# Six local attention layers: lower bound of the norms on ACT, rotation products stored head by head, and mix, output projection and MLP one unit later

## What is computed

```python
q, k, v = split(x_shifted @ Wqkv)
q = l2norm(q) * qs;  k = l2norm(k) * ks          # l2norm: t / max(|t|, 1e-12)
q = q * cos * scale + rotate_half(q) * sin * scale   # k with 1 / scale
p = softmax(8 * q @ k_near.T + mask)             # own window and the one before
x = x + (p @ v_near) @ Wo
xn = layernorm(x_shifted) * g + b
a, gate = split(xn @ W1 + b1)                    # 2 x 341
x = x + (a * gelu(gate)) @ W2 + b2
```

## Time and profile before

| | us |
|---|---|
| median of 3 runs | 3254.74 |
| lowest and highest | 3243.23, 3268.76 |
| profiled execution, its own time | 3245.79 |
| its span, first to last instruction | 3244.0 |
| PE busy in the span | 3124.8 (96%) |
| DVE busy | 3011.8 (93%) |
| POOL busy | 2636.1 (81%) |
| ACT busy | 2387.8 (74%) |

### The profile page before, as it was taken

One profiled execution on the slowest core, in us unless ns is written; L12 is line 12 of the kernel. 1 busy time (PEld: TensorE's weight loads), 2 busy tenths in 40 slices (PEclk: granted clock), 3 DMA queues, 4 the chain that ended last, 5 costly groups with the idle time before them and its releaser, 6 DMA issues.

```text
span 3244.0 us, 137191 instructions
## 1 busy us (share of the span) xinstructions
PE 3124.8 (96%) x59460; PEld 1936.9 (60%) x59460; DVE 3011.8 (93%) x3333; ACT 2387.8 (74%) x4288; POOL 2636.1 (81%) x1428
## 2 busy tenths in 40 slices
PE   7988999999999999999999999999999999998997
PEld 4555666666666666666666666666666666654554
DVE  6888999999999999999999999999999999965888
ACT  6875577777777777777777777777777777767896
POOL 1238889899898998899999989898999888963667
PEclk9998999999999999999999999999999999999999
DMA  3002344334444344343434443444433343350000
GB/s 99 2 1 67 119 126 129 114 118 124 121 129 128 119 124 122 121 127 117 126 119 129 124 127 114 123 119 128 128 119 117 119 121 118 119 158 1 2 11 18
DMA packets 237004, 336.45 MB, mean 104 GB/s; under 512 B 39926, under 2 KB 161140, under 8 KB 236020
## 3 DMA queue, kind: packets, MB, share of 16 engines
q1 hardware_dynamic: 236404, 327.69, 33.2%
HBM read 124.14 MB, written 102.76 MB: 70 GB/s over the span
## 4 chain that ended last, share of the span: by engine, by line
PE 83%; issue 5%; POOL 4%; DVE 4%; ACT 3%; DMA 0%; SPq 0%; POOLq 0%; DVEq 0%; ACTq 0%
PE psum L846 29%; PE psum L917 10%; PE psum L903 9%; PE psum L876 8%; PE psum L944 8%; PE psum L858 6%; PE psum L955 4%; PE psum L934 2%; PE psum L926 1%; ACT x_expo L1853 1%; POOL f_rotated L1433 1%; POOL f_rotated L1441 1%; ACT x_expo L420 1%; PE psum L1678 1%; PE psum L1688 1%
## 5 line engine op out<-in xcount | busy, mean ns | idle before, releaser
L1433 POOL TENSOR_TENSOR f_rotated<-f_times_cos,f_times_sin 128x1024 f32<-128x1024 f32 x384 | 908.2, 2365 | 2.9 <-DVE f_times_sin L1253 2.8
L1441 POOL TENSOR_TENSOR f_rotated<-f_rotated,f_rnorm 128x1024 f32<-128x1024 f32 x384 | 725.1, 1905 | 4.4 <-ACT f_rnorm L1081 4.4
L1090 ACT COPY f_qkT<-psum 128x1024 f32<-128x1024 f32 x384 | 370.7, 1015 | 370.2 <-PE psum L858 370.2
L1425 POOL TENSOR_TENSOR f_probs<-f_probs,f_rowsum 128x1024 f32<-128x1024 f32 x192 | 365.2, 1902 | 259.4 <-DVE f_rowsum L1294 256.5
L846 PE MATMUL psum<-w_qkv,f_xs 128*128 128x512 f32 x1152 | 529.5, 604 | 2.6 <-DVE f_times_sin L1253 1.0
L1070 ACT ACTIVATE f_squares<-psum 128x1024 f32<-128x1024 f32 x384 | 393.2, 1024 | 178.0 <-PE psum L846 173.2
L846 PE MATMUL psum<-w_next,f_xs 128*128 128x512 f32 x1152 | 522.6, 597 | 0.0
L1252 DVE TENSOR_TENSOR f_times_cos<-psum,f_rot 128x1024 f32<-128x1024 f32 x384 | 465.6, 1213 | 46.4 <-ACT f_squares L1070 45.5
L1253 DVE TENSOR_TENSOR f_times_sin<-psum,f_rot 128x1024 f32<-128x1024 f32 x384 | 464.3, 1209 | 0.0
L1260 DVE TENSOR_REDUCE f_sumsq<-f_squares 128x16 f32<-128x1024 f32 x384 | 454.0, 1183 | 0.2 <-issue 0.2
L846 PEld LDWEIGHTS psum<-w_qkv,f_xs 128*128 128x128 f32 x1152 | 217.5, 192 | 264.2 <-issue 257.4
(11 more groups left out here) (182 smaller groups left out, 5755.9 us busy)
## 6 DMA issues: line engine op xcount, KB each, us to landing
f_v_moved<-f_v SPq DMA_DIRECT2D x768, 128.0 KB
turned_blocks<-w_qkv SPq DMA_DIRECT2D x192, 512.0 KB, 2.6
f_probsT<-turned_blocks SPq DMA_DIRECT2D x768, 128.0 KB
w_qkv<-in_l_wqkv SPq DMA_DIRECT2D x36, 128.0 KB, 3.4
w_next<-in_l_wqkv SPq DMA_DIRECT2D x36, 128.0 KB, 2.4
w_o<-in_l_wo SPq DMA_DIRECT2D x6, 512.0 KB, 4.8
w_qkv<-in_ctxT SPq DMA_DIRECT2D x1, 2048.0 KB, 8.7
w<-in_l_w SPq DMA_DIRECT2D x6, 341.0 KB
```

Of the source, the lines that this page charges most:

```text
L1090: act.copy(qkT[u % 2][:, part].rearrange("p t (j n) -> p j t n", j=2), pair(("qT", "kT")[part], u).rearrange("p (j t n) -> p j t n", j=2, ...
L1433: pool.tensor_tensor(rotated[u % 2][:, part].rearrange("p h (s d) -> p s h d", s=2), halves(times_cos[part][:, :]), halves(times_sin[part] ...
L1441: pool.tensor_tensor(rt, rt, rnorm[u % 2][:, part * H:(part + 1) * H].unsqueeze(2).broadcast_to([P, H, HD]), ALU.mult).then_inc(normalised ...
```

## The change

Three edits, all in the local layers.

1. `clamp_norms` leaves DVE. `reciprocal_norms` on ACT waits for the two sums itself and computes `Relu(sum - 1e-24)`, then `Ln(that + 1e-24)`, then the `Exp` as before. Two one-column constants are set by POOL at the kernel's start.
2. `products` writes its two results in the order (head, half, 32) instead of (half, head, 32), and POOL's `rotate` adds them with plain rows of 1024 in and out.
3. Lags: mix 5 to 6, output projection 6 to 7, and each MLP stage one more, on PE, ACT, DVE and POOL; `load_out` and `load_mlp` on SP one step later; `ROTATING` and `END` follow; `mix(186)`, `project_out(185)`, `copy_mix(186)` and `add_out(185)` move from the loop to the written-out end. The lags of everything ahead of the mix, SP's `place_probs`, `place_v` and `store_probs` and ACT's `prepare` among them, stay.

```diff
+        norm_floor, under_floor = sb("norm_floor", [P, 1]), sb("under_floor", [P, 1])
...
-                act.wait_ge(eps_made, 1)
+                act.wait_ge(eps_made, 3)
...
-            ROTATING = (("q", 0, 1), ("up2", 13, GB), ("v", 4, 1), ("k", 0, 1), ("scores", 2, 1), ("up0", 11, GB), ("out", 6, 2),
-                        ("down", 13, GB), ("up1", 11, GB), ("qT", 1, 1), ("kT", 1, 1), ("mix", 5, 1), ("mean", 7, GB),
-                        ("variance", 9, GB))
+            ROTATING = (("q", 0, 1), ("up2", 14, GB), ("v", 4, 1), ("k", 0, 1), ("scores", 2, 1), ("up0", 12, GB), ("out", 7, 2),
+                        ("down", 14, GB), ("up1", 12, GB), ("qT", 1, 1), ("kT", 1, 1), ("mix", 6, 1), ("mean", 8, GB),
+                        ("variance", 10, GB))
...
-            END = (("up2", 44), ("v", 188), ("scores", 190), ("down", 44), ("kT", 191), ("qT", 191), ("v", 189), ("scores", 191),
+            END = (("mix", 186), ("up2", 44), ("v", 188), ("scores", 190), ("out", 92), ("down", 44), ("kT", 191), ("qT", 191), ("v", 189), ("scores", 191),
...
+            by_half = lambda t: t.rearrange("p (h s d) -> p s h d", s=2, h=H)
...
-                    if 0 < layer < DEPTH and into == 5:
+                    if 0 < layer < DEPTH and into == 6:
                         load_out(sp, layer)
-                    if 0 < layer < DEPTH and into == 12:
+                    if 0 < layer < DEPTH and into == 13:
                         load_mlp(sp, layer)
...
                 for step in range(2, UNITS):
                     project(step, 0)
-                    mlp_up(step - 13, 2)
+                    mlp_up(step - 14, 2)
                     project(step - 4, 2)
                     project(step, 1)
                     scores(step - 2)
-                    mlp_up(step - 11, 0)
-                    project_out(step - 6)
-                    mlp_down(step - 13)
-                    mlp_up(step - 11, 1)
+                    mlp_up(step - 12, 0)
+                    project_out(step - 7)
+                    mlp_down(step - 14)
+                    mlp_up(step - 12, 1)
                     transpose_qk(step - 1, 0)
                     transpose_qk(step - 1, 1)
-                    mix(step - 5)
-                    mlp_mean(step - 7)
-                    mlp_variance(step - 9)
+                    mix(step - 6)
+                    mlp_mean(step - 8)
+                    mlp_variance(step - 10)
+                mix(186)
                 mlp_up(179, 2)
                 project(188, 2)
                 scores(190)
+                project_out(185)
                 mlp_down(179)
...
                 def reciprocal_norms(u):
                     exp_tables()
-                    act.wait_ge(clamped, u + 1)
+                    act.wait_ge(summed[0], u + 1)
+                    act.wait_ge(summed[1], u + 1)
                     if u >= 2:
                         act.wait_ge(normalised[0], u - 1)
                         act.wait_ge(normalised[1], u - 1)
-                    act.activation(rnorm[u % 2][:, :], sumsq[u % 2][:, :], ACT.Ln).then_inc(norm_logged, 1)
+                    act.activation(rnorm[u % 2][:, :], sumsq[u % 2][:, :], ACT.Relu, bias=under_floor[:, 0:1]).then_inc(clamped, 1)
+                    act.wait_ge(clamped, u + 1)
+                    act.activation(rnorm[u % 2][:, :], rnorm[u % 2][:, :], ACT.Ln, bias=norm_floor[:, 0:1]).then_inc(norm_logged, 1)
...
-                    dve.tensor_tensor(halves(times_cos[part][:, :]), halves(taken), table(0), ALU.mult)
-                    dve.tensor_tensor(halves(times_sin[part][:, :]), halves(taken)[:, ::-1], table(1), ALU.mult).then_inc(producted[part], 1)
+                    dve.tensor_tensor(by_half(times_cos[part][:, :]), halves(taken), table(0), ALU.mult)
+                    dve.tensor_tensor(by_half(times_sin[part][:, :]), halves(taken)[:, ::-1], table(1), ALU.mult).then_inc(producted[part], 1)
...
-                def clamp_norms(u):
-                    dve.wait_ge(summed[0], u + 1)
-                    dve.wait_ge(summed[1], u + 1)
-                    dve.tensor_scalar(sumsq[u % 2][:, :], sumsq[u % 2][:, :], NORM_EPS2, None, ALU.max).then_inc(clamped, 1)
...
-                    pool.tensor_tensor(rotated[u % 2][:, part].rearrange("p h (s d) -> p s h d", s=2),
-                                       halves(times_cos[part][:, :]), halves(times_sin[part][:, :]), ALU.add).then_inc(rotations[part], 1)
+                    pool.tensor_tensor(rotated[u % 2][:, part].rearrange("p h d -> p (h d)"),
+                                       times_cos[part][:, :], times_sin[part][:, :], ALU.add).then_inc(rotations[part], 1)
...
+            pool.memset(norm_floor[:, :], NORM_EPS2).then_inc(eps_made, 1)
+            pool.memset(under_floor[:, :], -NORM_EPS2).then_inc(eps_made, 1)
```

More of the change, by code:

```diff
@@ L1174, in act @@
                 for step in range(2, UNITS):
-                    mlp_square(step - 9)
+                    mlp_square(step - 10)
                     square(step, 0)
                     reciprocal_norms(step - 1)
-                    mlp_gelu(step - 13, 2)
-                    mlp_affine(step - 11)
-                    mlp_root(step - 10)
+                    mlp_gelu(step - 14, 2)
+                    mlp_affine(step - 12)
+                    mlp_root(step - 11)
                     copy_v(step - 4)
@@ L1183, in act @@
                     exponentials(step - 4)
-                    mlp_gelu(step - 11, 0)
+                    mlp_gelu(step - 12, 0)
                     prepare(step + 1)
-                    mlp_gelu(step - 11, 1)
+                    mlp_gelu(step - 12, 1)
                     copy_qk(step - 1, 0)
                     copy_qk(step - 1, 1)
-                    copy_mix(step - 5)
-                    mlp_log(step - 9)
-                    mlp_shift(step - 6)
+                    copy_mix(step - 6)
+                    mlp_log(step - 10)
+                    mlp_shift(step - 7)
                 reciprocal_norms(191)
+                copy_mix(186)
                 exponentials(188)
@@ L1262, in sum_squares @@
                                       op=ALU.add).then_inc(summed[part], 1)
-                @each(UNITS)
-                def clamp_norms(u):
-                    dve.wait_ge(summed[0], u + 1)
-                    dve.wait_ge(summed[1], u + 1)
-                    dve.tensor_scalar(sumsq[u % 2][:, :], sumsq[u % 2][:, :], NORM_EPS2, None, ALU.max).then_inc(clamped, 1)
                 @each(UNITS)
@@ L1344, in dve @@
                 sum_squares(0, 1)
-                clamp_norms(0)
                 products(1, 0)
@@ L1350, in dve @@
                 sum_squares(1, 1)
-                clamp_norms(1)
                 for step in range(2, UNITS):
@@ L1354, in dve @@
                     sum_squares(step, 0)
-                    mlp_hidden(step - 13, 2)
+                    mlp_hidden(step - 14, 2)
                     products(step, 1)
                     mask_scores(step - 2)
[L1358 to L1361, removed]
+                    mlp_hidden(step - 12, 0)
+                    add_down(step - 14)
+                    mlp_hidden(step - 12, 1)
+                    add_out(step - 7)
                     row_sums(step - 4)
@@ L1365, in dve @@
                     turn_probs(step - 4)
-                    mlp_centre(step - 7)
-                    clamp_norms(step)
+                    mlp_centre(step - 8)
                 row_sums(188)
@@ L1371, in dve @@
                 row_maxima(190)
+                add_out(185)
                 add_down(179)
@@ L1464, in pool @@
                     normalise(step - 1, 0)
-                    mlp_scale(step - 10)
+                    mlp_scale(step - 11)
                     normalise(step - 1, 1)
```

## The result

| us | before | after |
|---|---|---|
| median of 20 runs | 3256.91 | 3238.38 |
| lowest to highest | 3243.23 to 3268.76 | 3230.6 to 3251.1 |
| profiled execution (span) | 3245.79 (3244.0) | 3230.85 (3229.0) |

The ratio after to before is 0.9948, with a 95% interval of 0.9937 to 0.9959. The change gains 0.5%, 18.5 us between the medians and 15.0 between the two profiled executions. The forecast was 14 us less, at 3241. The size of the sum came out well. Two of its terms did not, and the rest of this document is mostly about them.

The account below looks back on a forecast made before the run. PE's own work was taken as the floor in the steady part, with 12.9 us idle to win. Steady -11, start -3.8 and end +1 made -14 us, 3241 us set on the median; range 3225 to 3259.

Parts of the forecast that it names:

- What bounds the kernel: Steady part of the local layers: PE's own work sets 55.01 us per four steps; only its 12.9 us idle can be won.
- One unit later: Mix one step later on PE: placing DMAs get a step of slack, so L903's 9.3 us of waits go.
- The lower bound: Clamp from DVE to ACT: zero in the steady part (-1 to +2 us), but ends L917's 1.5 us of waits.
- The layout: Rotation on POOL and DVE: runs of 32 cost nothing, POOL's sum stays at 2365 ns, products at 1213; gain 0.
- The start: Bare steps before the MLP joins: 12.1 instead of 12.53 us without the clamp, -3 us taken, bounds 0 to 7.
- the swap: Start of the local layers: one bare step of 12.1 us added, one full step of 12.9 dropped, -0.8 us.
- The end: Behind the loop: mix(186) and project_out(185) add 5.2 us of PE work, mostly regained; +1 us taken, bounds 0 and +5.2.
- the cover: End of the local layers: project_out stands where PE idled 2.91 us ahead of the down projection, leaving +2.3 us.
- The waits stay: Rival, chance 0.15: L903's waits at the mix come from PSUM banks, not DMAs; only the start is won, 3252 us.
- POOL's sum gets cheaper: Rival, chance 0.12: runs of 32 cost POOL's sum 0.46 us; start gains 4 to 8 us more, 3235 us.
- ACT's gelu step fills up: Rival, chance 0.08: prepare falls between two gelus; beyond 0.9 us more lateness PE waits in 47 groups; 3288 at 1 over.
- The sum: Whole kernel: steady part -11, start -3.8, end +1 us give -14 us, bounds 0 and -20.

Follow-up runs that it names:

- the first experiment: The kernel before with the later mix, output projection and MLP alone, clamp and layout as before: 3238.93 against 3252.82 us, ratio 0.9954.
- the second profile: Profile of the changed kernel run once more, unaltered: profiled execution 3247.96 us; that run measured 3240.86 against 3255.27 us, ratio 0.9952.
- the second and seventh experiments: Kernel before, without the lags. Second: lower bound on ACT alone, ratio 0.9992. Seventh: bound on DVE as a reduction over pairs, ratio 0.9993.
- the third: The kernel before with the rotation products stored head by head alone: 3257.87 us, ratio 1.0006 to the kernel before.
- the sixth: The changed kernel with ACT's two prepare copies made twice in a row: 3264.37 us, ratio 1.0026 to the kernel before.
- eighth kernels: The kernel before with the later mix, output projection and MLP, plus the bound as a reduction on DVE, old layout: 3240.66 us, ratio 0.9948.

## Why the prediction was right, and where it was not

- **What bounds the kernel.** Right. PE is idle 5.2 of 2379 us (under 3 was forecast), four steps take 54.9 to 55.0, and freeing DVE by 5% of the steady part brought no more than its few waits.
- **One unit later.** Right in kind; the first experiment shows it alone. The step took L903's 9.3 us "as gone", and that was one kind too many. Its two rows mixed two things: waits ahead of the mix (7.3 us), which a later mix removes, and stops in the midst of its matmuls (2.0 us before, 4.1 after), which it does not. A look at which matmul record stands before each of the thirteen waits would have told them apart, and the steady term would have been 2 us smaller. The measured -10.6 hides this, because the pace of the matmuls was 0.1% better (3 us). That it met the forecast -11 is luck; the second profile has -7.7.
- **The lower bound.** The steady part's zero and the 1.5 us of L917 were right. The price of the Relu was not: it was taken as 0.23 us from an Ln without a bias tile, and with one it took 0.317, while the Ln rose from 0.229 to 0.323. ACT got 0.41 us per unit, not 0.23. That cost nothing, since ACT still had idle time. Whether it is why 0.7 us was left to spare and not 0.9 wasn't tried. The Trainium skill (ScalarE: Activation LUTs, Rules for kernel authors) says that a max or a relu belongs on VectorE. The runs agree only for a form that POOL doesn't hold: 947 ns for the clamp on DVE, 317 on ACT, 184 for the reduction on DVE. Once the lags are in, the time is the same with each of them within the intervals.
- **The layout.** Right: no change that the intervals show, alone or beside the other edits.
- **The start.** This is the term that was mis-sized: -3 with the swap's -0.8 beside it, measured -7.0 and -0.4 in the first profile (-4.3 and -0.4 in the second). The undisturbed bare steps did come out as forecast: POOL's L1425 stands at 281.48 and at 293.58, 12.10 us apart, where the earlier trace rows had 12.53. But the step counted only what the clamp's going frees, and left out that five bare steps also waited for the placing DMAs (3.0 us ahead of a mix; a sixth wait of 0.77 there is a stop). The lags remove those too. 3.0 + 0.8 + 3.0 = 6.8 lies between the two measured 7.4 and 4.7; that it is made up so is worked out and not measured apart. The clamp's 3 us are also not its own: without the lags the runs show no gain from it, in the second and seventh experiments. "Some steps are longer (mix waits...)" stood in the text as a source of doubt, where it should have been a term.
- **The end.** Right: +1.4 for +1, with the cover and the down projection's 2.6 us as worked out.
- **The rivals.** "The waits stay" fell to the first experiment and "POOL's sum gets cheaper" to the third. "ACT's gelu step fills up" did not happen, and the sixth shows that it would have from 0.7 us on.
- **The sum.** -14 was forecast for the profiled pair and -15.0 came; start 3.6 us more than forecast, steady part 0.4 less, end and rest 2.1 worse. The misses partly cancel, and a pair of profiled executions with the second profile would have shown no gain in the span at all (3246.2 against 3244.0). The medians of 20 runs, 18.5 us apart, are what bears the forecast out.

Open: why PE stops at these few of the places that lie 256 records apart. It comes in all kernels, and in the midst of a run no semaphore stands. In the steady part of those with the lags these stops add up to 1.9 to 8.4 us. At the stop of 1314.43 one 16 KB packet of the instruction queue was under way in the microsecond before it and took 9.6% of the 16 engines' microsecond, where such packets in a quiet stretch took 5.7 to 6.0%. The one ahead of the stop at 1441.74 took 6.0%. So a slow packet fits one case and not the other, and no run here changed the place or the number of these packets on purpose.

## What to carry to other kernels

Read each wait by what stands just before it on its engine. Here the waits ahead of the mix's first matmul were for its data and went with a step of slack, and those in the midst of its matmuls, where no semaphore stands, stayed. Where waits have no releaser, count the engine's records from one to the next: a common distance, 256 here, says more than their length. Where two resources race, relieving one alone can be worth nothing: freeing DVE alone showed no gain here, and the lags alone had the whole of it within the intervals. So the slack has to come first, and the two edits must be priced together. Before a small operation is moved to another engine because it is slow where it stands, look whether it is slow or held; another form of it on the same engine may not be held at all.

## What the runs showed of the hardware that I had not expected

- **A bias tile costs ACT 0.09 us.** 128x32 with a [128, 1] bias: 317 (Relu) and 323 ns (Ln). The same Ln without one: 229 before, 226 in the seventh kernel. The Ln with the bias also works in place, but that is not the price: the Exp behind it works in place too, without a bias, and takes 229 in the first and eighth kernels.
- **A maximum by reduction is not held behind POOL.** 184 ns mean over 192, against 947 for the tensor_scalar form of the same maximum, although it reads twice the columns.
- **PE's stops with no releaser keep to a grid.** All 47 stand whole multiples of 256 records apart in its list, and one instruction queue moved one 16 KB packet for each 256 records.
- **Two executions of one kernel differ by 17 us**, and about half of it is there before the local layers begin. The first stretch of the changed kernel's first profile, and then of its second:

```profile
0.00:228.00 228.00, 195.86 (x2284) 121.48 (x2316) 182.61 (x206) 177.59 (x654) 42.02 (x65) 1.00 0.12 36
```

```profile
0.00:228.00 228.00, 203.04 (x2258) 123.37 (x2260) 178.02 (x200) 173.10 (x635) 41.59 (x64) 0.97 0.12 36
```

The granted clock was 1.00 in the first and 0.97 in the second. The first local product started at 229.95 in the first; in the second it is this one:

```profile
238.78 1.23 DVE L1260 TENSOR_TENSOR f_times_cos<-psum,f_rot 128x1024 f32<-128x1024 f32 x1 [1.36 <-ACT f_squares L1074]
```

It is 8.8 us later, half of the 17.2 between the two spans. A gain of 15 us must be read from runs, or from stretches between the same events, never from two spans.
